# Expert tiles of the first four groups run inside the end chain of a Mamba and mixture-of-experts block

## The chip, the core and the metric

The kernel runs on one core of a Trainium2 chip. The metric is the device time of one execution in microseconds (us). The profile is one more execution, seen by the hardware profiler.

## The reference

Two sequences of 2048 tokens with 128 channels go through a bidirectional state-space layer and then a layer of eight experts, each with a layer norm before it and a gated residual after it:

```python
h = _layernorm(x) * (1 + ca) + sa
x = x + ga * attn(h)     # in_proj, causal conv + silu, scan, gate by silu(z), rms norm;
                         # forward and backward in time, summed, out_proj
h = _layernorm(x) * (1 + cb) + sb
top = argmax(h @ gate_w.T + gate_b + expert_bias)        # one expert per token
for e in range(8):
    y = relu(h @ w1[e] + b1[e]) @ w2[e] + b2[e]           # 128 -> 512 -> 128
    out = out + (top == e) * y
x = x + gb * out
```

Everything is float32. The chosen expert depends on the data, so which rows an expert gets is known only at run time.

## The kernel before, in words

Each engine has its own list of instructions, written out in order in one program; semaphores join the lists. An engine that waits holds up everything behind it on its own list.

*The scan.* Each sequence is scanned backward and then forward, 16 chunks of 128 tokens each way: 64 chunks (`NCH`), in 16 steps of four (`BT`). Step 15 is the last (`LAST`). A product of TensorE in float32 shows as two instructions in the trace.

*The groups.* Behind the forward steps, four chunks (512 tokens) at a time make a group, 0 to 7 (`LASTG` = 7). A group goes through: scaling and adding both directions (`forward` on ScalarE, `both` on VectorE), `y_turn`, `out_T`, `out_proj`, `residual`, the second norm (`second_deviation` on GpSimd, `second_norm` or, for group 7 in two halves, `half_norm` on VectorE), `h2_turn`, `second_T`, `logits`, `choose` (argmax), `ranks` (counts by matrix products) and `place`. `place(g)` leaves in `nextrow` the next free row of each expert's region in a DRAM buffer `routed_rows` (8192 rows for an expert) and in `rowat` the row of each token. `scatter(g)` on GpSimd then writes the group's rows (normed row, residual row, token number: 260 numbers) with four indirect transfers of 128 rows.

*The end chain.* When the last chunk is done, groups 5, 6 and 7 are still on their way. Their remaining steps are written out by hand: the TensorE list from `ranks(LASTG - 2)` to `ranks(LASTG)` has `keep_warm` products between the steps, which compute nothing that is used. VectorE ends with `place(LASTG)` and then a table of 39 slots (`NSLOT` = 32 + 7): for each expert the number of its tiles of 128 rows, their running sum, and from it for every slot the first row and the expert (`slot_r`). `s_tabv` says that the table is there. ScalarE then issues the first four loads of an expert's first weights (`w1b`, L1204), and SyncE, when all scatters have landed (`s_scat`), loads rows (L545) and later weights (L536).

*The expert stage.* For each of the 39 slots: SyncE loads 128 rows of 260 numbers into one of six buffers `rr` and the weights of its expert into one of four; `turn_rows` (TensorE, L1575) transposes the rows, `rows_T` (ScalarE, L1212) copies them, `hidden` (L1586) makes 4 x 128 hidden channels, `rectify_low` (ScalarE, L1220) and `rectify_high` (VectorE, L2172) apply bias and relu to a half each, `down` (L1597, L1603) reads the expert number into a register and makes the sum, `gates` and `combine` (VectorE) multiply by the sequence's gate and add the residual, and GpSimd reads the token numbers (`token_numbers`, L851) and stores with an indirect transfer (`put`, L856). The list of TensorE is turn(s+2), hidden(s+1), down(s).

*What orders the PSUM banks.* The group steps share banks 6 and 7 in the order of `side_order`; three late uses have a bank of their own (`OTHER`). Step 15's products use banks 0 to 5.

Of the kernel before, what the change touches and what calls it, by code (L numbers as in the profile page):

```python
# [14 lines left out]
P = 128  # L15
# [28 lines left out]
RR = 6  # L44
RW = 4
B2K = 96
# [55 lines left out]
def side_order():  # L102
# [44 lines left out]
    for key in (("rk", last - 2), ("h2", last - 1), ("lg", last - 1), ("h2", last, 0), ("rk", last - 1), ("h2", last, 1),  # L147
                ("lg", last), ("rk", last)):
        yield key
# [6 lines left out]
WARM_TABLE, WARM_SCATTER, WARM_ROWS = 18, 20, 6  # L156
# [4 lines left out]
OTHER = (0, 1, 2, 2, 3, 5, 4, 4)  # L161
for _bank, _key in enumerate((("yT", B * NBLK - 1, 1), ("o", B * NBLK - 1, 0), ("o", B * NBLK - 1, 1),
                              ("xT", 1), ("xT", 2), ("xT", 3), ("pfx", 0), ("erow", 0))):
    USE[_key] = LATE + _bank


def build(nc, u, w_xbc, w_zdt, conv_w, conv_b, dt_bias, a_log, d_skip, norm_w, w_out, gate_w, gate_b,
          w1, w2, b2, c_t, wmod, out):
    ctx = ExitStack()
    with ctx:  # L170
# [216 lines left out]
        s_tabv = sem("s_tabv")  # L387
        s_pad = sem("s_pad")
# [15 lines left out]
        s_ob = sem("s_ob")  # L404
        s_out = [sem(f"s_out{i}") for i in range(4)]

# [10 lines left out]
        NM = NTOK // P  # L417
        tiles_gt = over(NE * NM).rearrange("p (e m) -> p e m", e=NE)
        m128 = over(NM)
        ntile = over(NE)  # L420
        cum = over(NE)
        coef = over(NE)
        slot_i = over(NSLOT)
        behind = over(2 * NE * NSLOT).rearrange("p (k s e) -> p k s e", k=2, e=NE)
        slot_v = over(2 * NSLOT).rearrange("p (k s) -> p k s", k=2)
# [3 lines left out]
        rr = ZS[:, 0:RR * ROW].rearrange("p (a c) -> p a c", a=RR)  # L429
        w1b = ZS[:, RR * ROW:RR * ROW + RW * W1C].rearrange("p (a c) -> p a c", a=RW)  # L430
# [4 lines left out]
        gsel = over(2 * DM).rearrange("p (a c) -> p a c", a=2)  # L435
        tok = over(4).bitcast(mybir.dt.int32).rearrange("p (a c) -> p a c", a=4)
        yo2 = over(2 * DM).rearrange("p (a c) -> p a c", a=2)
        ob = over(4 * DM).rearrange("p (a c) -> p a c", a=4)

        SPARE = NE * REGION - P  # L440
# [47 lines left out]

        out_rows = out.rearrange("b t d -> (b t) d")
        LASTG = B * NBLK - 1  # L490
        NFILL0 = 6
        NCONST = 17
# [7 lines left out]
        def _(sp_):  # L500
# [25 lines left out]
            sp_.wait_ge(s_yz, NCH)  # L526
            sp_.wait_ge(s_tabv, 1)
# [4 lines left out]
            def load_w1(s, first):  # L532

                sp_.wait_ge(s_hra, s - RW + 1)
                sp_.wait_ge(s_hrb, s - RW + 1)
                sp_.dma_start(w1b[:, s % RW, :],  # L536
# [10 lines left out]
            first0, first1 = first_row(0), first_row(1)  # L547
            for a in range(RB):
# [1703 lines left out]
```

## Time and profile before

| | us |
|---|---|
| median of 3 runs (lowest, highest) | 446.13 (444.88, 448.41) |
| the profiled execution | 446.73 |
| its span, first to last instruction | 444.8 |
| TensorE products busy in the span | 400.8 (90%) |
| VectorE, ScalarE, GpSimd busy | 354.7, 290.8, 317.0 |
| mean granted clock of TensorE | 0.982 of 2.4 GHz |

The span is what the trace covers; 446.73 - 444.8 = 1.93 us lie around it. Busy shares are averages over stages with different limits, so each stage is read by itself. This is the part of the profile that shows the stages, 40 equal slices of 11.1 us; the digits are the busy tenths of a slice, PEclk the granted clock in tenths:

```profile
PE   7898989997998899798998998999988699999990
DVE  5758789998879999988889987996987078778781
ACT  3748699787699897787788789987420044444430
POOL 4744894899995989589898898697575245656662
PEclk9869999999999999999999999999999999999997
```

The scan runs to about slice 28, the end chain to slice 31, the expert stage from slice 32 on. The last slice holds the landing of the last stores.

### The profile page before, as it was taken

To read this page: it belongs to the slowest core of one execution; us is meant where nothing else is said; L and a number is where in the kernel's file an instruction comes from. 1 tells how busy PE (TensorE), PEld (TensorE's weight loads), DVE (VectorE), ACT (ScalarE), POOL (GpSimd) and SP (SyncE) were. 2 spreads that over 40 slices of the span, in tenths; PEclk is the share of its full clock that TensorE was granted. 3 is DMA by queue.
4 is the path that set the end of the run, shared out by engine and by line. 5 is a ranking of instruction groups with operands and counts; after the bars stand their busy time and mean duration, and the time that the engine had idled before them with its cause. 6 is when DMAs were issued, how large, how long until landed. Compare 5 with 4: busy or idle time off the path is not lost.

```text
span 444.8 us, 10736 instructions
## 1 busy us (share of the span) xinstructions
PE 400.8 (90%) x3156; PEld 364.5 (82%) x3156; DVE 354.7 (80%) x1064; ACT 290.8 (65%) x827; POOL 317.0 (71%) x478
## 2 busy tenths in 40 slices
PE   7898989997998899798998998999988699999990
PEld 7676878897898698587898887899877699999990
DVE  5758789998879999988889987996987078778781
ACT  3748699787699897787788789987420044444430
POOL 4744894899995989589898898697575245656662
PEclk9869999999999999999999999999999999999997
DMA  8999999999800000010101100031112578888740
GB/s 233 323 335 335 334 336 332 334 336 332 256 7 0 2 2 0 1 49 2 50 1 49 37 13 1 1 117 75 49 36 74 170 206 222 234 221 224 214 146 0
DMA packets 54856, 63.30 MB, mean 142 GB/s; under 512 B 4604, under 2 KB 47868, under 8 KB 54672
## 3 DMA queue, kind: packets, MB, share of 16 engines
q1 hardware_dynamic: 49808, 54.57, 41.4%
q0 software_dynamic: 2832, 6.50, 4.1%
q10 hardware_dynamic: 2160, 1.55, 1.3%
q8 instruction: 27, 0.44, 0.4%
q14 instruction: 29, 0.24, 0.2%
HBM read 20.97 MB, written 42.09 MB: 142 GB/s over the span
## 4 chain that ended last, share of the span: by engine, by line
PE 35%; DVE 17%; issue 12%; POOL 12%; ACT 10%; DMA 5%; SPq 5%; ACTq 2%; POOLq 0%; DVEq 0%
PE bank L1351 3%; PE bank L1302 3%; POOL out_dram L856 3%; PE bank L1367 3%; PE bank L1371 3%; PE bank L1344 3%; DVE bank L1778 3%; PE bank L1363 3%; POOL routed_rows L768 2%; PE bank L1329 2%; SPq L536 2%; POOL accb L637 2%; SPq L530 2%; DMA zs<-routed_rows 2%; PE bank L1335 2%
## 5 line engine op out<-in xcount | busy, mean ns | idle before, releaser
L637 POOL TENSOR_TENSOR accb<-accb,prod 128x512 f32<-128x512 f32 x48 | 61.3, 1278 | 29.2 <-ACT accb L949 25.5
L1778 DVE SCALAR_TENSOR_TENSOR bank<-raw,cw,bank 128x512 f32<-128x512 f32 x96 | 72.1, 751 | 2.3 <-ACT bank L959 0.9
L856 POOL DMA_INDIRECT out_dram<-raw x39 | 38.2, 979 | 34.3 <-POOL raw L851 12.8
L673 POOL TENSOR_SCALAR lseg<-strict,av 128x128 f32<-128x128 f32 x128 | 48.0, 388 | 6.8 <-DVE av L1737 4.8
L1351 PE MATMUL bank<-skip,cx 128*128 128x128 f32 x256 | 41.1, 283 | 7.0 <-DVE st L1824 6.6
L1212 ACT ACTIVATE raw<-bank 128x128 f32<-128x128 f32 x39 | 10.8, 278 | 53.4 <-PE bank L1575 47.8
L1239 PE MATMUL bank<-ones 128*128 128x128 f32 x266 | 38.8, 296 | 5.2 <-issue 2.7
L1603 PE MATMUL bank<-raw 128*128 x312 | 43.1, 282 | 0.0
L998 ACT ACTIVATE xt<-bank,dtv 128x128 f32<-128x128 f32 x128 | 39.5, 362 | 5.5 <-PE bank L1330 5.2
L768 POOL DMA_INDIRECT routed_rows<-rows,rowat x32 | 32.8, 1025 | 14.1 <-issue 8.6
L1351 PEld LDWEIGHTS bank<-skip,cx 128*128 128x128 f32 x256 | 33.6, 191 | 9.8 <-DVE st L1824 9.0
L1239 PEld LDWEIGHTS bank<-ones 128*128 128x128 f32 x266 | 35.8, 208 | 6.7 <-issue 5.4
L1586 PE MATMUL bank<-raw,zs 128*128 128x128 f32 x312 | 41.2, 275 | 0.0
L2172 DVE TENSOR_SCALAR raw<-bank,zs 128x128 f32<-128x128 f32 x78 | 23.8, 347 | 21.1 <-PE bank L1586 21.0
L1367 PE MATMUL bank<-xt,ms 128*128 128x128 f32 x256 | 39.0, 275 | 0.0
L1344 PE MATMUL bank<-incl,lseg 128*128 128x128 f32 x256 | 38.9, 274 | 0.0
L1603 PEld LDWEIGHTS bank<-raw 128*128 128x128 f32 x312 | 37.9, 192 | 0.5
L1371 PE MATMUL bank<-st,cs 128*128 128x256 f32 x128 | 38.2, 380 | 0.0
L1586 PEld LDWEIGHTS bank<-raw,zs 128*128 128x128 f32 x312 | 37.9, 192 | 0.0
L1363 PE MATMUL bank<-xt,bs 128*128 128x128 f32 x240 | 36.6, 275 | 0.0
L632 POOL TENSOR_SCALAR prod<-raw,cw 128x512 f32<-128x512 f32 x48 | 33.8, 705 | 3.8 <-ACT raw L907 2.7
L1811 DVE TENSOR_TENSOR ms<-es,bank 128x256 f32<-128x256 f32 x64 | 26.4, 412 | 9.6 <-ACT es L1010 9.0
(238 smaller groups left out, 1148.4 us busy)
## 6 DMA issues: line engine op xcount, KB each, us to landing
routed_rows<-padrow SPq DMA_DIRECT2D x32, 1040.0 KB, 12.6
zs<-in_w_dram SPq DMA_DIRECT2D x35, 258.0 KB, 3.3
zs<-routed_rows SPq DMA_DIRECT2D x39, 130.0 KB, 3.2
raw<-in_w_dram SPq DMA_DIRECT2D x1, 2048.0 KB, 7.6
xs<-in_u_dram SPq DMA_DIRECT2D x3, 512.0 KB, 9.7
routed_rows<-padrow SPq DMA_DIRECT2D x8, 130.0 KB, 3.4
zs<-in_w_dram ACTq DMA_DIRECT2D x4, 258.0 KB, 4.6
out_dram<-raw POOLq DMA_INDIRECT x39
```

Of the source, the lines that this page charges most:

```text
L637: pool.tensor_tensor(accb[:, :], accb[:, :], prod[:, :], ALU.add).then_inc(s_tapb, 1)
L673: last = pool.tensor_scalar(lseg[:, Q % LA, h, :], strict[:, d, :], av[:, b, col(d, h, t)], 1.0, ALU.mult, ALU.mult)
L856: pool.indirect_dma_start(out_rows, bass.IndirectOffsetOnAxis(ap=tok[:, s % 4, :].bitcast(mybir.dt.uint32), axis=0), ob[:, s % 4, :], None ...
L1239: pe.matmul(area[:, 0:P], ones[:, :], ones[:, :], start=True, stop=True, skip_group_check=True)
L1344: last = pe.matmul(sg[:, h * P:(h + 1) * P], lseg[:, Q % LA, h, :], incl[:, d, :], start=False, stop=True, skip_group_check=True)
L1351: last = pe.matmul(bank[4 + Q % 2][:, h * HD:(h + 1) * HD], cx[:, S % 2, h, c0:c0 + P], skip[:, d * NH + h, :], start=(h == 0), stop=False ...
L1363: pe.matmul(sn[:, h * HD:(h + 1) * HD], bs[:, Q % TM, h].rearrange("p g n -> p (g n)"), xt[:, Q % TM, h * HD:(h + 1) * HD], start=False, s ...
L1367: pe.matmul(ys[:, h * HD:(h + 1) * HD], ms[:, Q % 2, h, :], xt[:, Q % TM, h * HD:(h + 1) * HD], start=False, stop=False, skip_group_check= ...
L1371: pe.matmul(ys[:, 0:DI], cs[:, Q % 2, :], st[:, Q % 2, :], start=False, stop=True, skip_group_check=True).then_inc(s_ys, 1)
L1586: mm = pe.matmul(bank[2 + 2 * (s % 2) + f // 2][:, c0:c0 + P], w1b[:, s % RW, f * P:(f + 1) * P], hTs[:, s % 2, :], start=True, stop=True)
L1603: last = pe.matmul(y, hr[:, s % 2, f * P:(f + 1) * P], w2s[:, bass.ds(e, 1), f, :].rearrange("p a c -> p (a c)"), start=False, stop=(f == ...
L1778: dve.scalar_tensor_tensor(out=acc(S, g)[:, :], in0=raw[:, g, c0:c0 + BLK], scalar=cw[:, d, g, k:k + 1], in1=acc(S, g)[:, :], op0=ALU.mult ...
```

## The change

The expert slots are cut in two. `K1` = 9 is the number of complete tiles that four groups (2048 tokens) must contain whatever the choice: (4 x 512 - 8 x 127) / 128, rounded up. The first nine complete tiles are listed from `nextrow` after group 3, by a table on GpSimd in step 15 (`first_table`); a second piece on GpSimd (`taken_tiles`) works out from which tile of each expert the rest begins. These nine slots run between the steps of the end chain, in place of the `keep_warm` products. In them ScalarE rectifies both halves and copies each sum away (`keep_sum`), and VectorE applies gates and residual for all nine after the table (`first_gates`, `first_outputs`). GpSimd stores the nine after the last scatter. The remaining `K2` = 30 slots run as before once all scatters have landed, with 20 and 6 `keep_warm` products ahead of them. SyncE now issues all weights; there are 13 row buffers (`RR`); weights 0 to 2 of 4 lie in the dead buffer `hT`. Banks: turned rows and sums in 0 and 3, hidden channels in 4 and 5 or 1 and 2. `y_turn(LASTG, 1)` goes back into the shared banks.

```diff
+FIRSTG = 4
+K1 = -(-(FIRSTG * BLK - NE * (P - 1)) // P)
-RR = 6
+RR = 13
@@ SyncE
-            sp_.wait_ge(s_yz, NCH)
-            sp_.wait_ge(s_tabv, 1)
+            sp_.wait_ge(s_yz, CHUNKS + TPB + ZUSED)
...
+            sp_.wait_ge(s_firstv, 1)
+            landed(sp_, FIRSTG)
+            for s in range(K1):
+                first = first_row(s)
+                load_rows(s, first)
+                if s < RW:
+                    load_w1(s, first)
+            for s in range(RW, K1):
+                load_w1(s, first_row(s))
+            sp_.wait_ge(s_tabv, 1)
+            ahead = [first_row(s) for s in range(K1, K1 + 2)]
+            for s in range(K1, K1 + RW):
+                load_w1(s, ahead[s - K1] if s < K1 + 2 else first_row(s))
+            landed(sp_, B * NBLK)
...
@@ GpSimd
+            def first_table():
+                wide = [P, K1, NE]
+                first = prefix[:, 0, NE // 2:]
+                hold(pool, s_tab, NTAB0)
+                hold(pool, s_rt_dve, NR * (FIRSTG - 1) + 5)
+                link_first(pool.tensor_tensor(whole, nextrow[:, FIRSTG % 2, :], region_mid, ALU.subtract))
+                link_first(pool.tensor_scalar(whole, whole, 1.0 / P, ROUND, ALU.mult, ALU.add))
+                link_first(pool.tensor_scalar(first, whole, ROUND, 1.0, ALU.subtract, ALU.mult))
+                pool.tensor_scalar(coef[:, 0], first, -float(P), float(REGION), ALU.mult, ALU.add)
...
+                pool.tensor_copy(slot_r[:, :, 0:K1], last).then_inc(s_firstv, 1)
@@ step 15, chunk 2
+                        first_table()
                         forward_norms(LASTG, 0, 2)
                         scatter(g2)
@@ end
             scatter(LASTG - 2, 3, BT)
+            taken_tiles()
             scatter(LASTG - 1)
             scatter(LASTG)
+            for s in range(K1):
+                hold(pool, s_rb[s], 16)
+            pool.tensor_copy(tok1, rr[:, 0:K1, 2 * DM:2 * DM + 1]).then_inc(s_tok, K1)
+            for s in range(K1):
+                put(s)
@@ ScalarE
+            def rectify(s, half):
+                act.wait_ge(s_h1a if half == 0 else s_h1, s + 1)
...
+            def keep_sum(s):
+                act.wait_ge(s_y2, s + 1)
+                act.activation(ob1[:, s, :], sum_bank(s)[:, 0:DM], ACT.Copy).then_inc(s_yo2, 1)
             out_T(LASTG, 0)
+            rows_T(0)
+            rows_T(1)
             forward(LASTG, 2, BT)
+            rectify(0, 0)
+            rectify(0, 1)
             out_T(LASTG, 1)
+            rectify(1, 0)
+            rectify(1, 1)
             second_T(LASTG - 1)
+            rows_T(2)
+            keep_sum(0)
...
@@ TensorE
+            pe.wait_ge(s_firstv, 1)
+            turn_rows(0)
+            turn_rows(1)
             ranks(LASTG - 2)
+            hidden(0)
             out_proj(LASTG, 0)
             y_turn(LASTG, 1)
+            hidden(1)
             out_proj(LASTG, 1)
             h2_turn(LASTG - 1)
+            turn_rows(2)
+            down(0)
             logits(LASTG - 1)
+            hidden(2)
+            turn_rows(3)
+            down(1)
             h2_turn(LASTG, 0)
+            hidden(3)
             ranks(LASTG - 1)
+            turn_rows(4)
+            down(2)
             h2_turn(LASTG, 1)
             logits(LASTG)
+            hidden(4)
+            turn_rows(5)
+            down(3)
             ranks(LASTG)
+            NPE = 4
+            for s in range(NPE, K1):
+                if s + 1 < K1:
+                    hidden(s + 1)
+                    if s + 2 < K1:
+                        turn_rows(s + 2)
+                down(s)
+            pe.wait_ge(s_tabv, 1)
...
+            keep_warm(bank[high_low(K1 - 2)], WARM_SCATTER)
+            landed(pe, B * NBLK)
+            keep_warm(bank[high_low(K1 - 2)], WARM_ROWS)
+            turn_rows(K1)
+            turn_rows(K1 + 1)
+            hidden(K1)
+            for s in range(K1, NSLOT):
@@ VectorE
+                if g == FIRSTG + 1:
+                    dve.wait_ge(s_first, 1)
                 step(g, dve.tensor_tensor(nextrow[:, 1 - a, :], side(u)[:, V:V + NE], nextrow[:, a, :], ALU.add), 5)
...
+            first_gates()
+            first_outputs(0, K1 // 2)
+            first_outputs(K1 // 2, K1)
+            rectify_high(K1)
```

`landed(eng, groups)` waits for the scatters of so many groups. `ZUSED` = 16 is the number of 256-wide tiles of the buffer `zs` that the 13 row buffers and one weight buffer cover.

## Rows read from the trace of the kernel before

**Rows 1.** Windows of the expert stage: from:to, length, busy time (x instructions) of the engines, clock, DMA share, GB/s.
```profile
365.00:375.00 10.00, 10.00 (x93) 9.94 (x91) 8.05 (x30) 4.49 (x17) 6.26 (x10) 1.00 0.82 230
```

**Rows 2.** Timeline of the row transposes: start, length, engine, line, operation, tiles.
```profile
354.12 0.30 PE L1575 MATMUL bank<-ident,zs 128*128 128x128 f32 x1 [0.78 <-DMA zs<-routed_rows]
...
371.92 0.27 PE L1575 MATMUL bank<-ident,zs 128*128 128x128 f32 x1
...
373.93 0.27 PE L1575 MATMUL bank<-ident,zs 128*128 128x128 f32 x1
```

**Rows 3.** The chain that ended last, at the last scatters: start, length, what.
```profile
344.96 0.96 POOL routed_rows L768
...
346.23 5.44 DMA routed_rows<-rows,rowat
...
352.43 2.24 DMA zs<-routed_rows
```

**Rows 4.** Timeline of the end chain: last gate, ranks, scaling, norm, places, table, warming.
```profile
321.45 0.42 DVE L1844 TENSOR_TENSOR yzf<-bank,zs 128x256 f32<-128x256 f32 x1
...
323.51 0.18 PE L1429 MATMUL bank<-hot,strictb 128*128 128x32 bf16 x1 [0.30 <-DVE hot L1937]
...
323.98 0.91 ACT L1031 ACTIVATE yzf<-yzf,rn 128x256 f32<-128x256 f32 x2 [1.04 <-POOL rn L686]
...
325.72 1.33 DVE L1887 TENSOR_SCALAR rows<-rows,mv,rs 128x128 f32<-128x128 f32 x4
...
335.96 0.17 DVE L1956 CAST rowat<-posf 128x4 int32<-128x4 f32 x1
...
344.03 0.20 DVE L2159 CAST raw<-raw 128x78 int32<-128x78 f32 x1
...
344.38 4.70 PE L1239 MATMUL bank<-ones 128*128 128x128 f32 x40 [1.45 <-DVE raw L2159]
...
351.76 1.58 PE L1239 MATMUL bank<-ones 128*128 128x128 f32 x12 [2.67 <-issue]
```

**Rows 5.** Timeline of GpSimd and VectorE in step 15, small and 128x512 instructions.
```profile
314.71 0.19 POOL L683 TENSOR_SCALAR rt<-ssq 128x2 f32<-128x2 f32 x1 [5.82 <-ACT junk L1024]
...
314.99 0.72 POOL L686 TENSOR_TENSOR rn<-rt,mhalf 128x2 f32<-128x2 f32 x1
...
316.22 0.69 DVE L1891 TENSOR_TENSOR rows<-rows,row 128x512 f32<-128x512 f32 x1
```

**Rows 6.** Timeline of the queues that issue indexed loads: weights (zs<-in_w_dram) and rows.
```profile
345.30 4.26 ACTq L1204 DMA_DIRECT2D zs<-in_w_dram  x4
...
357.05 0.34 SPq L536 DMA_DIRECT2D zs<-in_w_dram  x1
...
358.15 0.33 SPq L545 DMA_DIRECT2D zs<-routed_rows  x1
...
358.88 0.34 SPq L536 DMA_DIRECT2D zs<-in_w_dram  x1
```

**Rows 7.** DMA issues of SyncE's weights: count, KB each, median us to landing.
```profile
zs<-in_w_dram SPq DMA_DIRECT2D x35, 258.0 KB, 3.3
```

**Rows 8.** Timeline of ScalarE in the expert stage: two quarters of a rectified slot.
```profile
355.53 0.63 ACT L1220 ACTIVATE raw<-bank,zs 128x128 f32<-128x128 f32 x2 [0.18 <-PE bank L1586]
```

**Rows 9.** Windows around the changes of the clock, columns as in rows 1.
```profile
18.20:19.50 1.30, 1.26 (x11) 1.26 (x12) 1.23 (x3) 1.30 (x5) 1.12 (x2) 1.00 1.09 334
...
19.60:25.60 6.00, 6.00 (x31) 6.00 (x29) 0.27 (x1) 1.32 (x3) 5.15 (x10) 0.50 1.09 333
25.60:29.70 4.10, 4.10 (x7) 1.90 (x7) 3.10 (x14) 2.87 (x5) 0.81 (x1) 0.50 1.09 336
...
349.10:351.70 2.60, 0.00 (x0) 0.00 (x0) 0.00 (x0) 0.00 (x0) 0.00 (x0) 1.00 0.77 232
434.40:439.30 4.90, 0.00 (x0) 0.00 (x0) 0.79 (x3) 0.00 (x0) 1.95 (x2) 1.00 0.01 0
439.40:444.80 5.40, 0.00 (x0) 0.00 (x0) 0.00 (x0) 0.00 (x0) 0.00 (x0) 0.50 0.00 0
```

More of the change, by code:

```diff
@@ L146, in side_order @@
     last = B * NBLK - 1
-    for key in (("rk", last - 2), ("h2", last - 1), ("lg", last - 1), ("h2", last, 0), ("rk", last - 1), ("h2", last, 1),
+    for key in (("rk", last - 2), ("yT", last, 1), ("h2", last - 1), ("lg", last - 1), ("h2", last, 0), ("rk", last - 1), ("h2", last, 1),
                 ("lg", last), ("rk", last)):
@@ L487, in take, with turn_bank, sum_bank, high_low @@
                 eng.wait_ge(s_free[u % 2], u // 2)
+        def turn_bank(s):
+            return bank[0] if s % 2 == 0 else bank[3]
+        def sum_bank(s):
+            return turn_bank(s + 1) if s < K1 else bank[6 + s % 2]
+        def high_low(s):
+            return 4 if s < 3 or s % 2 == 0 else 1
+        def same_banks(s):
+            return s - 1 if s in (1, 2) else s - 2
+        def landed(eng, groups):
+            for a in range(RB):
+                eng.wait_ge(s_scat[a], 64 * ((groups - a + RB - 1) // RB))
         out_rows = out.rearrange("b t d -> (b t) d")
@@ L1224, in _ @@
+            def keep_sum(s):
+                act.wait_ge(s_y2, s + 1)
+                act.activation(ob1[:, s, :], sum_bank(s)[:, 0:DM], ACT.Copy).then_inc(s_yo2, 1)
+            out_T(LASTG, 0)
             rows_T(0)
             rows_T(1)
-            rectify_low(0)
-            for s in range(NSLOT):
+            forward(LASTG, 2, BT)
+            rectify(0, 0)
+            rectify(0, 1)
+            out_T(LASTG, 1)
+            rectify(1, 0)
+            rectify(1, 1)
+            second_T(LASTG - 1)
@@ new lines, in _ @@
+            rows_T(2)
+            keep_sum(0)
+            rectify(2, 0)
+            rows_T(3)
+            rectify(2, 1)
+            keep_sum(1)
+            second_T(LASTG, 0)
+            rectify(3, 0)
+            rectify(3, 1)
+            rows_T(4)
+            keep_sum(2)
+            second_T(LASTG, 1)
+            NACT = 3
+            for s in range(NACT, K1):
+                if s + 1 < K1:
+                    rectify(s + 1, 0)
+                    if s + 2 < K1:
+                        rows_T(s + 2)
+                    rectify(s + 1, 1)
+                keep_sum(s)
@@ L1228, in _ @@
+            rows_T(K1)
+            rows_T(K1 + 1)
+            rectify(K1, 0)
+            for s in range(K1, NSLOT):
                 if s + 2 < NSLOT:
```

294 lines of the change are left out of this document (175 added, 119 removed).

## The prediction, made before the result

> **What bounds the kernel now.** I read the 40 slices first, for where each engine is full, then the windows of the last stage, then the timeline of what stands in front of it. The last stage is the expert stage, 39 slots of 128 rows. In it TensorE is busy 10.00 us of 10.00 and a slot takes 373.93 - 371.92 = 2.01 us from one row transpose to the next [rows 1, 2]: TensorE alone sets that pace. The stage begins at 354.12, when the first rows have landed [rows 2].
>
> What sets this beginning is the end chain from 321.9 on. The trace's chain of waits for it runs through GpSimd: eight scatters 1.27 us apart, the last starting at 346.23, 5.44 us until it has landed, then the load of the first rows, 2.24 us [rows 3]. The eight wait at their head for the place numbers of group 6, ready at 336.13; TensorE, ScalarE and VectorE work towards them in short steps, TensorE filling its waits with warming products [rows 4]. So in 322 to 354 TensorE is busy, but little of that is needed, and 9 slots x 2.01 = 18 us would fit in.
>
> **The change, part by part.**
>
> *Nine slots leave the last stage.* 30 slots stay, with the same 18 or so TensorE instructions each. Gain 9 x 2.01 = **-18.1 us**, on the path for all of it, since the stage is bound by TensorE.
>
> *The first table on GpSimd* is some 18 small instructions, most linked to the one before. The nearest rows are 0.19 us for a small instruction and 0.09 to the one linked to it [rows 5]; wider operands take somewhat more: about 5.5 us. With four more constants before it (0.9 us) it fits between 308.9 and 315.4; GpSimd idled 5.82 us there, to 314.71. It delays the norms by 0.7 us and group 4's scatters by as much, and nobody waits for those: ScalarE takes up the norms only at 316.5. The place step of group 5 also waits for its first instruction, done some 13 us before it. Cost 0; were the cover gone, the 0.7 us. `taken_tiles`, six more after the last scatter of group 5, lies in GpSimd's idle 333.4 to 337.1: 0.
>
> *SyncE's loads* wait for s_yz of CHUNKS + TPB + ZUSED = 32 + 16 + 16 = 64, which is all 64 chunks: nothing is loaded before the last gate, 321.45 + 0.42 = 321.87 [rows 4]. From the end of the table's last instruction, 344.03 + 0.20 [rows 4], to the first indexed load, 345.30 [rows 6], took 1.07 us on ScalarE, so rows 0 start at about 323.0. SyncE's spacing is 0.73 us from rows to weights and 1.10 from weights to rows [rows 6]: rows 1 start at 324.85 and land 2.24 us later, at **327.1**. The weights of 0 started at 323.7 and land by 327 (3.3 us is the median [rows 7]). SyncE then stays ahead: weights 4 start at about 335.6, which slot 4 needs at 341.
>
> *What queues behind rows 1.* On TensorE `turn_rows(0)` and `turn_rows(1)` stand ahead of the ranks of group 5, which ran at 323.51 [rows 4]; now 327.25, **+3.75 us**. On ScalarE `rows_T(1)` stands ahead of the scaling of the last half block, 323.98 before, 327.75 now. VectorE waits for both, GpSimd for VectorE's place numbers. I carried the engines' new lists forward with the durations of the rows and with 1.0 us a product group (8 instructions), 0.63 a rectified half [rows 8], 0.28 a ScalarE copy. TensorE at the full clock: ranks 327.25 to 327.6, `hidden(0)` to 328.5, output product to 329.4, transposes 329.7 to 330.3, `hidden(1)` to 331.2, second output product to 332.2, group 6's transposes 332.5 to 333.1, `down(0)` to 334.2, group 6's logits to 335.1. VectorE: places of 5 done 328.7, sum of the half block 329.6, second norm of group 6 from 329.65 (325.72 before) to 332.4, the two residual halves to 334.7, first half norm to 336.3, choice of group 6 to 337.6, second half norm to 339.0, places of 6 done 340.0 (336.13). So TensorE's inserted groups mostly end before VectorE asks. Places of 7 are done at 344.2, which GpSimd asks for only at 345.1. The shift stays **+3.9 us** at GpSimd, so the last scatter lands at 351.67 + 3.9 = 355.6. The ninth slot's product ends at 351.9, the 20 + 6 warming products (4.70 us for 20, 1.58 for 6 [rows 4]) at 357.9, as rows 9 land at 358.0: both sides are ready together, and **every further delay of TensorE counts in full**.
>
> *The clock.* TensorE has one transpose between 322.3 and 327.1, where 12 warming products stood. With nothing between 349.1 and 351.7 it stayed at 1.00, the level of 2.4 GHz; among short and 2-column products it fell at 19.5 to 0.50, 1.2 GHz; after the end of work at 434.3 it fell near 439.3, 5 us later [rows 9]. A 4.8 us pause with one transpose is nearest to the last, so I take it as falling. How long low: the wide, unbroken products from 25.6 on ran low to 29.7, where it rose [rows 9], 4.1 us; I take 4 to 5 us from 327.2, so 2.2 us of TensorE work lost. The bounds: nothing, and the 10.2 us of 19.5 to 29.7, 5 us lost. With 2.2 us lost, the transposes of the last half block, its output product and group 6's logits come about 2 us later still, VectorE's half norms 0.9 later, group 6's places at 341.9, scatters end at 352.9 and land at 357.4. The ninth slot ends at 354.6, warming at 360.4: TensorE is now last. The first transpose of the rest is at 360.5 against 354.12: **+6.4 us**.
>
> The Trainium skill, "TensorE: Matmul & The Clock Gate", section "Why this matters for your kernels", says that a pause of TensorE between bursts of matmuls brings the low clock back; section "Part 4: PE-mode transpose" says that transposes do not count as busy. The trace agrees for the pause of 5 us and has no row for one transpose within a pause. By it the sum is 435.3; without it 432.8.
>
> *Phase 2's start.* Nine stores go out before the tenth, about 1.27 us each on GpSimd as the scatters are [rows 3], against 2.01 for a slot; GpSimd is about 3 us late and catches up in four slots, with four output buffers. VectorE's work for them (twice 128x1152 and four passes of 128x512 to 128x640, at 0.69 for 512 [rows 5]) is about 6 us, done by 357, needed from 362. Cost 0 to 0.8; I take 0.2 for rows 9 sharing the transfers. Weights 9 to 12 are issued by SyncE instead of ScalarE, 1.1 us apart after the table, before the scatters land: 0.
>
> *Sum.* 444.8 - 18.1 + 6.4 + 0.2 = 433.3 of span; with the 1.93 us that the profiled run has around its span (446.73 - 444.8), **435.3**. That run is 0.6 above the median of the three, so I say 435.0.
>
> **The rivals.**
>
> A. *The clock holds.* For it: no drop in the 2.6 us pause. Against: the pause is nearly twice as long. The last stage starts at 358.2 instead of 360.7: 432.8.
>
> B. *The interleaving is stickier.* Each `down` reads its expert number from memory into a register; in the full stage TensorE's queue hides that, in the chain the queue is often empty. The nearest price is the 1.07 us from semaphore to issue, about half of it the read. Nine times 0.5 us, after the ninth slot counts in full: 435.3 + 4.5 = 439.8. Against: the first two slots of the last stage show no gap at L1597. It also stands for ScalarE, whose slot is 1.26 + 0.28 + 0.28 = 1.82 us of 2.01.
>
> C. *Slower: the clock stays low through the nine slots.* Place: TensorE from 327.2 to the ninth `down`, about 25 us of work at the full clock. Low throughout it takes 50, the ninth slot ends near 378, and with warming at the low clock the rest starts at 383 to 389: 457 to 463. It decides from some 22 us of low clock on, for 11 us net gain at half a microsecond each. For it: 10 us low in the first 30 us, with short and 2-column products between. Against: from 327 TensorE has a backlog of full-width products, which should lift it.
>
> D. *It does not do what it says*: the nine are not through when the scatters land, or they stall on loads. Rows are in order on every engine, so it shows as B, only longer; 442 to 446.
>
> **How the numbers follow.** Forecast 0.52, own range 433 to 438 (from 2 us less low clock and a last scatter that lands faster than 5.44, to the longer low stretch). A 0.22, B 0.16, C 0.05, D 0.05. The likeliest is the forecast, 435.0. A range from 431 (A, landing 1.5 us faster) to 441 (B with a longer low stretch) leaves out C, D and ends: 0.12 or so. What can be told from no change is 1%, 441.7 to 450.6: faster has forecast, A and nearly all of B, 0.88; same D and a rest, 0.06; slower C and a rest, 0.06.
>
> **What would show it.** In the changed trace: 30 transposes at 2.01 us in the last stage; SyncE's first rows at about 323.0 and the ranks of group 5 at about 327.2; a granted clock of 0.50 for some 4 to 5 us from before 330; TensorE without a pause of over 1 us from 336 to 354; the first transpose of the last stage at about 360.5, right behind the warming products. If it waits for rows instead, the scatters set the start. The prediction is wrong if the nine slots take over 2.3 us each, if the clock falls more than once, or if rows 1 land later than 328.

## The result, and the profile after

The changed kernel took 442.04 us (median of four, 440.08 to 444.38), the kernel before 446.75 beside it: a ratio of 0.989, with a 95% interval of 0.985 to 0.993. The forecast was 435.0, with an own range of 433 to 438 and a wider one of 431 to 441; the result lies outside both. The change is faster, but by 4.7 us (1.1%) and not by the 11 of the forecast, and it lies inside the 441.7 to 450.6 that the forecast counted as no clear change. The profiled run took 444.38 us, its span is 442.6.

The gain is in the place that was forecast, and it is lost again, most of it in one place. The timeline of TensorE where the rest of the slots begins, start, length, engine, line, operation, tiles and in brackets the idle time ahead and who ended it:

```profile
354.96 5.97 PE L1382 MATMUL bank<-ones 128*128 128x128 f32 x52
360.76 0.38 PE L1688 MATMUL bank<-ident,zs 128*128 128x128 f32 x2
368.29 2.07 PE L1705 MATMUL bank<-raw,hT 128*128 128x128 f32 x8 [7.14 <-ACT raw L1319]
370.16 0.42 PE L1688 MATMUL bank<-ident,zs 128*128 128x128 f32 x1
370.37 1.91 PE L1705 MATMUL bank<-raw,hT 128*128 128x128 f32 x8
```

ScalarE in the same stretch:

```profile
355.16 0.28 ACT L1335 ACTIVATE yzb<-bank 128x128 f32<-128x128 f32 x1 [1.06 <-PE bank L1726]
367.96 0.45 ACT L1319 ACTIVATE raw<-bank 128x128 f32<-128x128 f32 x2 [12.53 <-remote]
```

GpSimd in the same stretch, the first and the last of the nine early stores:

```profile
354.96 1.01 POOL L970 DMA_INDIRECT out_dram<-yzb,raw  x1 [2.28 <-DVE yzb L2348]
...
365.22 0.97 POOL L970 DMA_INDIRECT out_dram<-yzb,raw  x1 [0.30 <-issue]
366.18 0.33 POOL L963 CAST raw<-zs 128x1 int32<-128x1 f32 x2
```

The first transposes of the rest stood at 360.76, against the 360.5 that the forecast gave; but this execution had its last gate add at 318.32, 3.1 us earlier than the kernel before, and counted from there it is 42.4 us against 39.05, so that the agreement is luck. And ScalarE got their result only at 367.96, 7 us later. The trace calls the releaser "remote" because it holds no signal that released the wait; by the program this copy waits for two semaphores, and TensorE alone raises both. That is 1.8 us behind the end of the last early store. TensorE stood still, and its clock fell. Windows of the two pauses of TensorE and what followed each, columns as in [rows 1]:

```profile
319.18:321.30 2.12, 0.00 (x0) 0.00 (x0) 0.85 (x5) 0.70 (x3) 1.93 (x4) 1.00 0.40 124
321.30:328.05 6.75, 4.50 (x26) 4.17 (x27) 3.17 (x12) 2.60 (x8) 1.39 (x3) 0.50 0.74 187
...
360.90:365.80 4.90, 0.25 (x3) 0.01 (x1) 0.00 (x0) 0.00 (x0) 3.68 (x5) 0.99 0.26 85
365.80:373.20 7.40, 4.91 (x26) 4.85 (x27) 1.45 (x6) 1.97 (x7) 0.71 (x3) 0.55 0.14 40
```

So in this stretch it fell twice: behind the last gate, as forecast, and again at the start of the rest. More than one fall was a sign that the forecast had named for being wrong.

**A measure that leaves the head out.** The moment of the last gate add moves by several us between executions of one kernel (316.6 to 320.9 in five profiles of the changed one). I therefore count a **tail**: the span less the start of that add. The kernel before has 444.8 - 321.45 = 123.4 [rows 4], the changed one here 442.6 - 318.32 = 124.3, where the forecast gave 433.3 - 321.45 = 111.9. By its tail this execution gained nothing; the rest of its difference is in the head. Of the 12.4 us above the forecast, 3.4 lie ahead of the first transposes of the rest, and 9.0 behind them: 442.6 - 360.76 = 81.8 in place of 72.8.

### The profile page after: what moved, and what is told of

Same layout as the page of the kernel before. It is cut to its first block and busy times, and to the rows that moved or that the text cites. A ratio compares the mean times of both kernels' runs of the same rounds, so it can differ in the third digit from the quotient of the medians.

```text
span 442.6 us, 10519 instructions
## 1 busy us (share of the span) xinstructions
PE 392.0 (89%) x3056; PEld 356.7 (81%) x3056; DVE 345.1 (78%) x1016; ACT 296.8 (67%) x854; POOL 323.0 (73%) x494
## 5 line engine op out<-in xcount | busy, mean ns | idle before, releaser
L970 POOL DMA_INDIRECT out_dram<-raw x30 | 29.2, 975 | 31.1 <-DVE raw L2381 12.1
L873 POOL DMA_INDIRECT routed_rows<-rows,rowat x32 | 34.0, 1062 | 17.8 <-issue 8.1
L1705 PE MATMUL bank<-raw,hT 128*128 128x128 f32 x240 | 35.0, 292 | 8.2 <-ACT raw L1319 8.2
L1705 PEld LDWEIGHTS bank<-raw,hT 128*128 128x128 f32 x240 | 31.6, 205 | 8.8 <-ACT raw L1319 8.6
L688 POOL TENSOR_SCALAR prod<-raw,cw 128x512 f32<-128x512 f32 x48 | 34.2, 712 | 3.8 <-ACT raw L1026 2.7
L1506 PE MATMUL bank<-xt,bs 128*128 128x128 f32 x240 | 36.6, 275 | 0.0
L1510 PEld LDWEIGHTS bank<-xt,ms 128*128 128x128 f32 x256 | 34.2, 194 | 0.0
L1487 PEld LDWEIGHTS bank<-incl,lseg 128*128 128x128 f32 x256 | 33.8, 192 | 0.0
L1120 ACT ACTIVATE bs<-bank,etab 128x64 f32<-128x64 f32 x128 | 33.3, 320 | 0.0
```

Source lines behind the costliest of these rows:

```text
L688: pool.tensor_scalar(prod[:, :], raw[:, NH, c0:c0 + BLK], cw[:, d, NH, k:k + 1], 1.0, ALU.mult, ALU.mult).then_inc(s_prod, 1)
L1487: last = pe.matmul(sg[:, h * P:(h + 1) * P], lseg[:, Q % LA, h, :], incl[:, d, :], start=False, stop=True, skip_group_check=True)
L1506: pe.matmul(sn[:, h * HD:(h + 1) * HD], bs[:, Q % TM, h].rearrange("p g n -> p (g n)"), xt[:, Q % TM, h * HD:(h + 1) * HD], start=False, s ...
L1510: pe.matmul(ys[:, h * HD:(h + 1) * HD], ms[:, Q % 2, h, :], xt[:, Q % TM, h * HD:(h + 1) * HD], start=False, stop=False, skip_group_check= ...
L1705: mm = pe.matmul(bank[high_low(s) + f // 2][:, c0:c0 + P], w1t[s % RW][:, f * P:(f + 1) * P], hTs[:, s % 2, :], start=True, stop=True)
```

## The experiments

The kernels of a set ran one after the other on one chip, and each set had its own runs of the kernel before.

| set | kernel | median us | ratio to before, interval | tail us |
|---|---|---|---|---|
| first | changed | 442.04 | 0.989, 0.985 to 0.993 | 124.3 |
| I | x1 changed | 433.74 | 0.972, 0.968 to 0.977 | 111.4 |
| I | x2 no early stores | 432.66 | 0.970, 0.966 to 0.974 | 110.4 |
| I | x3 early loads | 428.94 | 0.961, 0.958 to 0.965 | 108.5 |
| I | x4 warmed waits | 433.43 | 0.970, 0.966 to 0.974 | 111.8 |
| II | x5 changed | 446.49 | 0.996, 0.992 to 1.000 | 123.5 |
| II | x6 14 warming products | 441.88 | 0.985, 0.980 to 0.989 | 120.3 |
| II | x7 seven slots first | 440.16 | 0.981, 0.977 to 0.986 | 119.0 |
| II | x8 early loads, 14 products | 441.90 | 0.987, 0.979 to 0.994 | 115.8 |
| III | x9 before (one run) | 449.00 | | 125.8 |
| III | x10 changed | 444.27 | 0.994, 0.989 to 0.999 | 125.2 |
| III | x11 no register read | 443.64 | 0.990, 0.984 to 0.996 | 123.6 |
| III | x12 no warming products | 441.86 | 0.985, 0.981 to 0.989 | 121.0 |
| IV | x13 no early stores | 432.18 | 0.972, 0.965 to 0.980 | 110.5 |
| IV | x14 stores spread | 433.46 | 0.975, 0.968 to 0.982 | 111.1 |
| IV | x15 early loads, 14 products, stores spread | 427.56 | 0.962, 0.955 to 0.969 | 105.5 |
| IV | x16 changed | 432.80 | 0.974, 0.966 to 0.982 | 111.3 |
| V | x17 stores spread | 433.11 | 0.973, 0.966 to 0.981 | 110.9 |
| VI | x18 as x15 | 426.80 | 0.961, 0.955 to 0.967 | 105.1 |

The kernel before had 446.38, 448.21, 448.21, 444.18, 444.43 and 445.52 us in sets I to VI.

### The same kernel again: x1, x5, x10, x16

No edit.

> The changed kernel once more. In its first profile the start of the last stage came as forecast (the transposes of rows 9 and 10 issued at 360.8), but ScalarE took them up only at 368.0, 7.2 us later; the profile also shows completions of TensorE late by 1.6 to 3 us near 341 and near 349. Theory 1 (the stall belongs to the program: something that always runs there blocks TensorE's completions): the same gap of 5 to 8 us behind the transposes of rows 9 and 10 again, time 440 to 444. Theory 2 (a disturbance of that one execution): the gap is under 1 us or sits elsewhere, and the median still is 440 to 442 by other waits.

> The changed kernel word for word, a third time. In its first measurement it took 442.04 us, with a ratio of 0.989 to the kernel before; in the second 433.74 us, with a ratio of 0.972. Theory S (the first measurement had a stall of its own: the two transposes ahead of the tenth slot stood at 360.76 and ScalarE took their result 7 us later; the program doesn't hold it): 432 to 436 us here, a ratio of 0.967 to 0.977, and hidden(9) within 1 us of the transposes. Theory T (the program has the stall in a share of its executions whatever the session): single executions at both levels, some near 434 and some near 442. Theory U (the second session was the odd one): 440 to 444 us again, and hidden(9) 6 to 8 us behind the transposes.

> The changed kernel word for word, as the reference of its set. So far 442.04, 433.74 and 446.49 us in three sets, beside 446.75, 446.38 and 448.21 us of the kernel before. Theory S: 432 to 436 us if no wait on TensorE of over 2 us stands behind 341 us in its profile, 440 to 448 us if they do.

> The changed kernel word for word, as the reference of its set: over 440 us if its profile has ScalarE's wait of 12 us ahead of the tenth slot, 432 to 436 if not.

433.74, 446.49, 444.27 and 432.80 us. In x1 and x16 the late result is gone; x1's TensorE at the same place:

```profile
353.29 5.97 PE L1382 MATMUL bank<-ones 128*128 128x128 f32 x52
359.09 0.38 PE L1688 MATMUL bank<-ident,zs 128*128 128x128 f32 x2
359.73 1.16 PE L1705 MATMUL bank<-raw,hT 128*128 128x128 f32 x8 [0.26 <-ACT raw L1319]
```

In x10 it is back, with two shorter ones ahead of it. ScalarE, then VectorE of x10:

```profile
343.71 0.62 ACT L1328 ACTIVATE raw<-bank,hT 128x128 f32<-128x128 f32 x2 [2.00 <-remote]
350.75 0.28 ACT L1319 ACTIVATE raw<-bank 128x128 f32<-128x128 f32 x1 [2.27 <-remote]
367.43 0.45 ACT L1319 ACTIVATE raw<-bank 128x128 f32<-128x128 f32 x2 [12.66 <-remote]
```

```profile
343.65 0.17 DVE L2111 TENSOR_TENSOR nextrow<-bank,nextrow 128x8 f32<-128x8 f32 x1 [3.99 <-remote]
```

Theory T (both levels mixed within a set) falls: a set is of one sort, the first, II and III with late results, I and IV without. The chip doesn't decide it either: sets I and III ran on the same one. In tails, x10 is 125.2 - 111.4 = 13.8 us behind x1. Counted from the last gate add, the warming products start at 37.7 in place of 34.2 (+3.5, the two waits of 2 us behind scatters), `hidden(9)` at 51.2 in place of 40.6 (+7.1 more), and the stretch from there to the end takes 74.0 in place of 70.8 (+3.2, the low clock among it). x5 and the first result have the same pattern, with ScalarE's wait of 12.62 and 12.53.

It is not only the signals that come late. TensorE itself stops among instructions that wait for nothing, in x5 among the warming products ("issue" says that nothing in the trace ended the idle time):

```profile
365.17 0.27 PE L1382 MATMUL bank<-ones 128*128 128x128 f32 x1 [1.05 <-issue]
```

And on GpSimd the last scatter takes 1.89 or 1.90 us in seven of the eight traces of the changed kernel and its variants with late results and 1.63 in the eighth (x7), against 0.96 in every trace without them. In x9 it takes 0.96.

### The kernel before: x9

No edit.

> The kernel before word for word, for its profile beside the changed one in the same set of runs. Open is whether the late completions of TensorE (2 to 7 us, behind 341 us) belong to the chip of a set or to the changed kernel. Theory S (the chip delays TensorE whatever runs): in a set in which the changed kernel takes over 440 us, this profile too has a wait of ScalarE or VectorE on TensorE of over 2 us that the earlier profile of the kernel before doesn't have. Theory K (only the changed kernel's mix brings it out): none here, 445 to 449 us, and the rows of the end as in the earlier profile.

Neither theory as I put it. ScalarE and VectorE have no such wait, but TensorE does stop among the warming products of the kernel before, which the earlier profile doesn't show there [rows 4]. TensorE of x9:

```profile
344.22 1.59 PE L1239 MATMUL bank<-ones 128*128 128x128 f32 x10 [1.43 <-DVE raw L2159]
346.96 0.27 PE L1239 MATMUL bank<-ones 128*128 128x128 f32 x1 [1.15 <-issue]
347.68 0.27 PE L1239 MATMUL bank<-ones 128*128 128x128 f32 x1 [0.45 <-issue]
348.42 6.27 PE L1239 MATMUL bank<-ones 128*128 128x128 f32 x40 [0.47 <-issue]
```

It ends 1.4 us behind the last of eight scatters (346.06 + 0.96). There TensorE only fills time until the rows land, so the kernel before pays little: its rest starts 0.5 us later. The changed kernel has put work there that others wait for. The other 1.9 us by which x9's tail is longer lie inside its rest, where four slots take 2.3 to 3.0 us.

### The early stores: x2, x13, x14, x17

Left out (x2, x13), and spread over the rest (x14, x17):

```diff
-            for s in range(K1):
-                put(s)
...
-            hold(pool, s_put1, 16 * K1)
```

```diff
-            for s in range(K1):
-                put(s)
+            early = list(range(K1))
             for s in range(K1, NSLOT):
                 token_numbers(s)
                 if s > K1:
                     put(s - 1)
+                    if (s - K1) % 3 == 0 and early:
+                        put(early.pop(0))
+            assert not early
```

> The nine early slots are computed but never stored (their rows of the output are missing). Theory 1a: GpSimd's nine indirect stores in a row, 355 to 366, hold up TensorE's completions: without them the gap behind the transposes of rows 9 and 10 falls under 1 us, the clock does not drop there, and the time is 7 to 10 us less, 432 to 434. Theory 1b, the gap has another cause: it stays, and the time is within 2 us of the changed kernel.

> The nine early stores are left out (those rows of the output stay unwritten). In the set in which the changed kernel took 433.7 us this took 432.7. Theory B (where late completions exist, TensorE's completions are held while GpSimd issues a burst of indirect DMAs: the transposes ahead of the tenth slot were given free 1.9 us behind the ninth store's end in each such profile): if the changed kernel beside it takes over 440 us, this one is 8 to 11 us faster than it, and the 12 us wait of ScalarE is gone; the 2 us wait behind the four scatters stays. Theory M (the total traffic or the time since the start is the cause): within 3 us of the changed kernel, with a wait of 5 us or more near 366. If the changed kernel takes 434 beside it, both theories say 432 to 434.

> The same nine early stores, one behind every third store of the rest in place of all nine in one burst ahead of them; nothing is left out. GpSimd has 0.76 us free in each slot of the rest (2.0 us), 2.3 in three slots, and a store takes 1.28. Theory B: if the changed kernel beside it takes over 440 us, 8 to 11 us faster than it; the ScalarE wait ahead of the tenth slot falls from 12 to some 6 us. Theory M (the count of packets is what matters, and it is the same here): within 3 us of the changed kernel. Theory G (GpSimd falls behind in the rest and becomes the bound): 3 us or more slower than the kernel without the stores, with ScalarE or VectorE waiting for s_out. If the changed kernel takes 434 beside it, Theory B and M both say 433 to 435.

> The spread stores again, nothing left out. A set with late completions shows in the profile by waits of 2 us of ScalarE and VectorE behind the burst of four scatters near 343. If it is one: Theory B (the burst of nine stores holds TensorE's completions) says 435 to 439 us and a ratio to the kernel before of 0.975 to 0.982, with ScalarE's wait ahead of the tenth slot near 6 us; Theory M (the total is what matters) says 441 to 446 and a ratio of 0.985 or more. If it isn't one, both say a ratio of 0.970 to 0.978.

All four fell in sets without late results. There the nine stores cost 1.1 us (x2 against x1) and 0.6 (x13 against x16), 1.0 and 0.8 by tail, less than the 2 to 5 us by which the executions of one kernel differ. Spreading them takes 0.2 to 0.4 off the tail, though by its median x14 is 0.7 above x16; GpSimd doesn't fall behind, so theory G falls. The question they were made for, whether the burst of nine stores holds TensorE's results back, none of them could answer.

What speaks for it is the order of events. In all eight profiles of the changed kernel and its variants with late results (first, x5 to x8, x10 to x12) the last long wait ends 1.3 to 1.9 us behind the end of the last early store, although the rest begins at different times in them. VectorE of x12, whose transposes ran at 361.80:

```profile
364.72 0.61 DVE L2358 TENSOR_SCALAR raw<-bank,hT 128x128 f32<-128x128 f32 x2 [6.06 <-PE bank L1705]
370.46 0.61 DVE L2358 TENSOR_SCALAR raw<-bank,hT 128x128 f32<-128x128 f32 x2 [5.13 <-remote]
```

and GpSimd's last early store there:

```profile
367.88 0.97 POOL L970 DMA_INDIRECT out_dram<-yzb,raw  x1 [0.30 <-issue]
```

Against a simple rule: x12's results came through at 364.7, when the burst had run since 357.05. And the shorter waits fit it less well: the second of them ends 0.7 us ahead of the end of the last scatter in x10 (350.75 against 351.40) and 0.8 in the first result, and x11's first on VectorE ends 0.5 ahead of the end of its first four scatters.

### The loads ahead of the last gates: x3

```diff
-            sp_.wait_ge(s_yz, CHUNKS + TPB + ZUSED)
+            sp_.wait_ge(s_yz, CHUNKS + TPB + ZUSED - BT)
```

> SyncE's first loads wait for 60 gates and not for all 64 (the last buffer that they overwrite is read by gate 60). My account of the beginning: rows 0 and 1 land before TensorE is free, the pause of TensorE from 319 to 324 and the low clock after it go, the ranks of group 5 stand near 320.5 instead of 324.3: 3.7 us from the queue and about 2.4 us from the clock, 5 to 6 us less than the changed kernel, 435 to 437. If scatters or other waits set the start of the last stage instead: under 2 us less.

428.94 us, 4.8 below x1, just short of the 5 to 6 expected. The low clock did not go, but it lasted 3.4 us in place of 6.8. TensorE of x1, then of x3:

```profile
325.47 0.47 PE L1688 MATMUL bank<-ident,zs 128*128 128x128 f32 x1 [2.48 <-DMA zs<-routed_rows]
325.74 0.23 PE L1572 MATMUL bank<-hot,strictb 128*128 128x32 bf16 x1
```

```profile
317.79 0.38 PE L1688 MATMUL bank<-ident,zs 128*128 128x128 f32 x2
319.10 0.18 PE L1572 MATMUL bank<-hot,strictb 128*128 128x32 bf16 x1 [0.92 <-DVE hot L2098]
```

The ranks come 6.62 us behind the start of the last gate add in x1 (319.12), 2.00 in x3 (317.10), 2.06 before [rows 4]. The ninth slot ends at 30.1 us behind it in place of 34.2, which gives 4.1; two later waits of TensorE on rows took 1.2 of it back in the profiled run.

### Warming products in the first waits: x4

```diff
+            pe.wait_ge(s_yz, NCH)
+            keep_warm(bank[4], 11)
             turn_rows(0)
+            keep_warm(bank[4], 8)
             turn_rows(1)
```

> 11 warming products before the transpose of rows 0 and 8 before that of rows 1, in time in which TensorE only waits. By my account the clock holds at 1.00 from 319 to 361 and the transposes of rows 9 and 10 come 2 us sooner: time 1.5 to 2.5 us less than the changed kernel. If the low clock cost nothing that the waits did not hide, no difference (under 0.5 us).

The clock stayed at 1.00 and the first `hidden` took 1.14 us, against 2.05 in x3 and in the first result. Yet the time is 433.43 against 433.74, and the ninth slot ends 33.9 us behind the last gate add against 34.2. The clock drop that I priced at 2.2 us costs 0.3 by the place of the ninth slot, and in the times nothing that stands out of their spread. For comparison x1, at the low clock and behind it:

```profile
322.98:329.78 6.80, 4.32 (x28) 4.25 (x28) 3.43 (x12) 2.60 (x8) 1.31 (x2) 0.50 0.75 211
329.78:335.00 5.22, 5.22 (x47) 5.12 (x47) 4.68 (x18) 2.68 (x8) 4.31 (x7) 1.00 0.71 196
```

It is low for 6.8 us, and TensorE is busy in only 4.32 of them. The waits around it take up the loss: at the transposes of group 6 x4 is 1.3 us ahead of x1 (11.5 against 12.8 us behind the last gate add), and then it waits 0.7 ahead of the first `down` where x1 doesn't.

### Warming products ahead of the rest, and the first phase's size: x6, x7, x8, x12

```diff
-WARM_SCATTER, WARM_ROWS = 20, 6
+WARM_SCATTER, WARM_ROWS = 8, 6
```

x12 has 0, 0 there. x7 has

```diff
-K1 = -(-(FIRSTG * BLK - NE * (P - 1)) // P)
+K1 = 7
```

and x8 is x3 and x6 together.

> Twelve of the 26 warming products ahead of the tenth slot are left out (WARM_SCATTER 20 to 8); all else as in the changed kernel. Theory A (the warming products are the last thing ahead of the rest: in the execution at 432.19 us they ran 353.29 to 359.09, at 0.223 us each, while SyncE issued the tenth slot's rows at 353.78 and they landed 2.6 us later, 356.4): the rest starts 2.6 us earlier, 2.4 to 2.7 us faster than the changed kernel beside it (some 431 us). Theory B (the rows of the tenth and eleventh slot land only when the products are over): the same time, and TensorE waits on a DMA ahead of the transposes. Theory C (the clock falls for want of the products): 1 us or more slower, with granted clock below 1 behind 356.

> Seven slots in the first phase in place of nine (K1 = 7); the rest runs 32 slots in place of 30. Theory A (each slot in the rest costs 2.01 us; the rest can't start before the rows that SyncE asks for behind the last scatter, 353.8 + 2.6 us, and the 26 warming products, 5.8 us, start behind the seventh slot, near 349): the rest starts at 356.4 in place of 359.1, which gives 2.7 us back, and the two slots more cost 4.0: 1.3 us slower than the changed kernel beside it (435 us). Theory B (the start of the rest is tied to the ninth slot alone, 2.0 us a slot): the rest starts 2 x 2 us or more earlier, and the time is the same within 1 us. Theory C (the start of the rest doesn't move): 4 us slower.

> SyncE starts the first phase's loads four gates of the last step early (s_yz at 60 in place of 64; 428.94 us alone, 4.8 below the changed kernel), and WARM_SCATTER is 8 in place of 20. Theory A (the two gains lie in different stretches and add): 4.8 + 2.6 us below the changed kernel, 426.3 us. Theory B (with the early loads the last scatter's landing bounds the rest): in the profile of the early loads alone SyncE asked for the tenth slot's rows at 347.7, 0.5 us behind the ninth slot's end, so the second gain is at most 2.7 us and falls to 0 where the row loads take over 5 us: 428.9.

> All 26 warming products ahead of the tenth slot are left out. Theory A (they are the last thing ahead of the rest and they hold the clock): the rest starts 2.7 us earlier, with the rows' landing, but TensorE stands still for 3 us ahead of it, its clock falls to 0.50 for some 4 us as it did behind the last gate, and 2 us go back: within 1.5 us of the changed kernel. Theory P (in the sets with late completions, a backlog of TensorE that these 52 instructions add to is what ScalarE waits out, 12.6 us behind them): in such a set 5 us or more faster than the changed kernel. Theory N (the backlog has another cause): in such a set the late completion moves to the tenth or eleventh slot, as it did with 14 products, and the time is within 2 us of the 14 products' gain, 4.6 us.

All four fell in sets with late results, so their small steps are mixed with those. x6 is 4.6 us below x5 (3.2 by tail), more than theory A said. x12 is 2.4 below x10: its transposes waited 5.23 us for rows, the clock fell, and the late result moved to the next slot as theory N said, 5.13 us on VectorE. The gain falls 0.2 us short of the band that N gave, and it is too large for theory A and too small for P. x7 is 6.3 us below x5 where theory A said 1.3 above: with seven stores the burst ends earlier, and so does the last wait (369.14, 1.3 us behind the last store). That is a miss, and it fits the burst, but seven slots also change all else in front. x8 is no faster than x6 by its median, 4.5 us by its tail.

### No register read in the first phase: x11

```diff
-                e = pe.value_load(slot_r[0:1, 1, s:s + 1], min_val=0, max_val=NE - 1)
+                e = 0 if s < K1 else pe.value_load(slot_r[0:1, 1, s:s + 1], min_val=0, max_val=NE - 1)
```

> In the first phase TensorE doesn't read the slot's expert from the table and takes expert 0's second weights and bias for all nine slots (so its result differs for those slots); the products are as many as before, without the register read ahead of each. Theory A (the read costs what its gaps show, 0.49 and 0.33 us ahead of two slots in the execution at 432.19 us, under 0.3 elsewhere): within 1 us of the changed kernel beside it. Theory B (rival B of the forecast: 0.5 us in each of nine slots): 3 to 4.5 us faster. Theory R (the register reads bring on the late completions in the sets that have them; a gap of 0.84 us stood ahead of the fourth slot's read there): in such a set 8 to 12 us faster than the changed kernel beside it, and no wait of 2 us on TensorE in the profile.

443.64 us against 444.27, and 1.6 less by tail: theory A by the median. The register reads neither cost 0.5 us a slot (my rival B) nor bring on the late results: ScalarE's wait of 12.11 us is there.

### The best version: x15 and x18

x3's early loads, x6's 14 products and x14's spread stores together.

> SyncE's early start (s_yz at 60), 14 in place of 26 warming products, and the early stores spread over the rest. Theory B: 424 to 428 us in a set without late completions (434 - 4.8 - 2.6), and 428 to 434 in one with them, where the first waits of 2 us behind the scatters stay. Theory M: 438 to 441 in a set with late completions, as x8 (441.9) which had the burst.

> The best version again. If its profile has the waits of 2 us on TensorE behind the four scatters near 343 (a set with late completions): Theory B (the burst of nine stores) says 430 to 435 us and a ratio to the kernel before of 0.963 to 0.973, where the same kernel with the burst had 441.9 us and 0.987; Theory M (the total) says 439 us or more. If it has none, both say 426 to 429 us, a ratio near 0.962.

427.56 us, 5.2 below the changed kernel beside it, and 426.80: faster than both kernels. TensorE of x15 at the start of the rest:

```profile
349.17 3.29 PE L1384 MATMUL bank<-ones 128*128 128x128 f32 x28
352.37 0.33 PE L1690 MATMUL bank<-ident,zs 128*128 128x128 f32 x1
352.97 0.33 PE L1690 MATMUL bank<-ident,zs 128*128 128x128 f32 x1 [0.27 <-DMA zs<-routed_rows]
353.13 1.09 PE L1707 MATMUL bank<-raw,hT 128*128 128x128 f32 x8
```

`hidden(9)` starts 33.9 us behind the last gate add (319.19), 36.6 in x3 with 26 products: 2.6 us, what theory A of x6 said, and the rows now land just behind the products. Both fell in sets without late results, so what it does in the others is unknown.

## Why the prediction was right and wrong, by its own steps

- **Nine slots leave the last stage, 2.01 us each: right.** The rest runs at that pace in x1:

```profile
365.00:375.00 10.00, 10.00 (x93) 9.94 (x92) 8.00 (x30) 4.52 (x15) 6.57 (x12) 1.00 0.87 236
```

- **First table hidden: right.** In the first result it ran from 306.57 to 312.0, and GpSimd had the norms ready at 313.1; ScalarE took them up at 313.38 without having waited.

```profile
306.57 0.21 POOL L777 TENSOR_TENSOR raw<-nextrow,raw 128x8 f32<-128x8 f32 x1
...
311.79 0.20 POOL L799 CAST raw<-raw 128x18 int32<-128x18 f32 x1
```

- **SyncE's loads behind all gates: right in place and spacing, short by up to 0.9 us.** SyncE's first rows in x1 start 1.00 us behind the end of the last gate add (319.54), where 1.1 was forecast from [rows 6], and rows 1 follow 1.83 later as forecast. But rows 1 took 3.10 us to the transpose that waits for them, not the 2.24 of [rows 3]. That is the longest of the 14 profiles in which the loads wait for all gates: they have 2.2 to 3.1, 2.43 in the first result. x1:

```profile
320.54 0.36 SPq L593 DMA_DIRECT2D zs<-routed_rows  x1
321.26 0.34 SPq L584 DMA_DIRECT2D hT<-in_w_dram  x1
322.37 0.34 SPq L593 DMA_DIRECT2D zs<-routed_rows  x1
```

- **What queues behind rows 1: right, and shown by x3.** Forecast +3.75 for the ranks; 5.95 - 2.06 = 3.9 in the first result and 6.62 - 2.06 = 4.6 in x1, the difference being that landing.
- **The clock: the fall was right, its length and price weren't.** 6.8 us low in place of 4 to 5 (as in eleven other profiles in which the loads wait for all gates; 10.2 in x10), and 0.3 us lost in place of 2.2 (x4). I counted TensorE's lost work as the path, where the engines around it had the slack. The Trainium skill, "TensorE: Matmul & The Clock Gate", section "Why this matters for your kernels", says that a pause brings the low clock back; the trace agrees, with 0.50 from 2.9 us behind the last product of x1 ahead of the pause on. The price can't be had from it.
- **Start of the rest: right to 0.9 us for TensorE, by luck.** Forecast 39.05 us behind the last gate add, 39.97 in x1, behind the warming products and not the rows. The forecast put the end of the ninth slot 33.15 us behind the last gate add, 2.7 of it for the clock; x4, whose clock held, needs 33.9. So the interleaved slots took some 2.9 us more than the lists that I had carried forward (0.6 of landing aside), a term that I had at nothing and that the clock's price happened to cover. Part of it can be seen: the `down` steps of the fifth to seventh slot of x1 start 2.77 and 2.61 us apart in place of 2.01 (343.89, 346.66, 349.27), over the 2.3 that I had named as a sign of being wrong. Where the rest of it went is open. x1:

```profile
346.66 0.23 PE L1720 MATMUL bank<-b2p,b2one 96*128 x1 [0.49 <-issue]
```

- **The rest from there: 1.4 us shorter than forecast.** 433.3 - 360.5 = 72.8 against 430.5 - 359.09 = 71.4. One slot of the kernel before had taken 2.95 us (its transposes at 388.12 and 391.07), and I had carried that over. The last sums have small slips too: 433.3 + 1.93 is 435.2, and 0.6 less is 434.6, not 435.0.
- **Phase 2's start: the step that failed.** I wrote "Cost 0 to 0.8" for the nine stores and what stands around them, and took it that ScalarE has the transposes as soon as they are done. In sets without late results that holds: 0.6 to 1.1 us. In the first result, and in II and III, results of TensorE reached ScalarE and VectorE 2 us late twice and, where 26 warming products and nine slots stand ahead, 5.8 to 7.3 us late at this place. In the first result it was 7.2, and from these transposes to the end it took 81.8 us in place of 72.8. Neither [rows 2] nor any other row of the kernel before shows it, since its first profile has no late result, and x9 shows that there they would fall among warming products that nobody waits for.
- **The rivals.** A's time (432.8) came out in sets I and IV, but not by its mechanism: the clock did fall. B's time (439.8) is 2.2 below the first result; x11 rules its price of 0.5 us a slot out, though the interleaving was stickier than I had it, as said above. D's 442 to 446 takes in the first result, 442.04, but not by its mechanism: the nine slots were through at 354.96, and the transposes of the rest followed the warming products without a wait for rows. C didn't occur.

So of the 442.04 us, about 434 go by the forecast's steps and are repeated in two sets, with the 2.9 us of the interleaved slots seen only in part, and the rest is the late results. **What causes those stays open.** Shown is where they stand, that they belong to a set of runs and not to the kernel or the chip alone, and that they cost the changed kernel 12 to 14 us of tail and the kernel before 2.4. That GpSimd's bursts of indirect DMAs hold them back is argued from their timing; the runs that would have shown it fell in other sets. The traces with late results also hold fewer signal records (4,286 to 4,522, against 5,651 to 5,802 in all others). Most of the missing ones tell of DMA landings, and they are missing long before the first late result: every trace has 960 of these up to 160 us, but between 180 and 300 us those with late results have 105 to 122 and the others 254 to 272, x9 among the former. So what sets such a set apart is there from 180 us on, in both kernels, while the first result that is 2 us late comes behind 340. Whether the recording itself holds the engines up, or only suffers from the same cause, no run here tests.

## What to carry to other kernels

Filling a waiting engine with real work takes away its cover: a delay that fell among warming products before now counts in full, so ask what the filler hid besides the wait you know. Before you explain a loss by a mechanism of the kernel, run the same kernel in another set: here its median moved by 13.7 us while that of the kernel before moved by 4.0. Where a queue waits for a count of all units, look at which of them its transfer really needs; here four fewer gave 4.8 us.

## What the runs showed of the hardware

- The same program, on the same chip, has two levels from set to set: 433.74 and 444.27 us, with the results of TensorE 2 to 7 us late in the second. The last of eight back-to-back scatters took 0.96 us in the first and 1.90 in the second.
- A clock drop of 6.8 us cost 0.3 us at most, by the place of the ninth slot, in a stretch where TensorE was busy 64% of the time. The low stretches behind the last gate were 3.4, 6.8 or 10.2 us long (x3 and x18 the first, x10 the last, the others that had one 6.8).
- An indexed row load of 130 KB, with a 258 KB weight load issued ahead of it, took 2.2 to 3.1 us from its issue to the transpose that waits for it in 14 profiles; in the kernel before one landed in 2.24.
- The start of an execution varies: the last gate add of the changed kernel began between 316.6 and 320.9 us in five profiles.
